# A graph layer with linear attention and routed experts: preparation and layers joined in one block, five of 49 tiles aggregated earlier

## The reference, cut to what matters

```python
xn = layernorm(x)
# graph branch
h   = xn @ W_gcn
deg = segment_sum(edge_weight, dst) + 1;  dinv = rsqrt(deg)
agg = segment_sum(dinv[src] * w * dinv[dst] * h[src], dst) + dinv**2 * h
g   = relu(0.5 * (layernorm(agg + b) * gamma + beta) + 0.5 * xn)
# linear attention, 8 heads
q, k, v = elu(xn@Wq)+1, elu(xn@Wk)+1, xn@Wv
att = (q @ (k.T @ v)) / (q @ k.sum(0)) @ Wproj + bproj
x1  = x + g + att
# 16 experts, the best two of each node, a last layernorm, and the residual
out = x1 + layernorm(xh + moe(xh)),  xh = layernorm(x1)
```

## Time and profile before

| what | value |
|---|---|
| median of 3 runs | 1736.85 us (1732.56 to 1738.45) |
| the profiled execution's own time | 1734.48 us |
| its span, first to last instruction | 1732.2 us |
| TensorE busy, its weight loads, VectorE, ScalarE, GpSimd | 84%, 70%, 59%, 29%, 58% |
| mean granted TensorE clock | 0.903 of full speed |
| first gather issued, last gather issued | 133.63 us, 1183.12 us |

### The profile page before, as it was taken

The page is one execution under the profiler, slowest core; times in us unless marked ns, Lnnn a source line. Parts: engine busy times, 40 slices in busy tenths (PEclk is TensorE's granted clock), DMA queues, the critical chain, the costliest instruction groups (busy, mean ns, idle before and its releaser), DMA issues. The chain is left out here.

```text
span 1732.2 us, 31432 instructions
## 1 busy us (share of the span) xinstructions
PE 1451.3 (84%) x8024; PEld 1205.2 (70%) x8025; DVE 1025.7 (59%) x3853; ACT 504.7 (29%) x1380; POOL 999.4 (58%) x1058
## 2 busy tenths in 40 slices
PE   5779979887968787977888869868499999999996
PEld 3668867665757565766666657645299999989975
DVE  8866367446367553852755528436755555566658
ACT  1346622121212111211111202101444444444424
POOL 0007037777777777777777777772045554545547
PEclk8889989897979888899888988878799999999998
DMA  7445113333333333333333333333932233254267
GB/s 241 157 149 183 59 44 104 106 105 104 107 104 104 107 104 107 104 106 105 107 104 107 104 107 104 106 105 92 216 113 77 71 123 97 73 170 149 76 216 279
DMA packets 107070, 207.62 MB, mean 120 GB/s; under 512 B 24496, under 2 KB 60080, under 8 KB 106960
## 3 DMA queue, kind: packets, MB, share of 16 engines
q0 software_dynamic: 48240, 131.91, 26.2%
q1 hardware_dynamic: 58720, 74.37, 14.0%
HBM read 172.60 MB, written 33.60 MB: 119 GB/s over the span
## 5 line engine op out<-in xcount | busy, mean ns | idle before, releaser
L137 POOL DMA_INDIRECT ring<-table,src x782 | 746.0, 954 | 437.7 <-issue 220.9
L1167 PE MATMUL bank<-ring,hots 128*128 x1372 | 321.7, 390 | 40.0 <-SPq L824 40.0
L1167 PEld LDWEIGHTS bank<-ring,hots 128*128 128x128 f32 x1372 | 264.5, 195 | 88.4 <-issue 51.8
L1674 ACT ACTIVATE one<-bank,b 128x128 f32<-128x128 f32 x424 | 155.5, 367 | 217.4 <-PE bank L1701 193.8
L1167 PE MATMUL bank<-ring,late_hots 128*128 x384 | 136.8, 508 | 93.4 <-SPq L824 87.0
L1701 PEld LDWEIGHTS bank<-one,w 128*128 128x128 f32 x1696 | 207.0, 193 | 8.1 <-issue 2.0
L1701 PE MATMUL bank<-one,w 128*128 128x128 f32 x1696 | 208.1, 276 | 1.3 <-issue 0.7
L1709 PE MATMUL bank<-w,one 128*128 128x256 f32 x848 | 202.8, 382 | 1.7 <-DVE y L1773 1.7
L1620 POOL DMA_INDIRECT spread<-y,to_x x109 | 107.2, 983 | 162.1 <-DMA spread<-y,to_x 82.9
L993 DVE TENSOR_SCALAR hots<-iota_t,edge_l 128x128 f32<-128x128 f32 x686 | 183.0, 362 | 1.8
L1167 PEld LDWEIGHTS bank<-ring,late_hots 128*128 128x128 f32 x384 | 91.0, 250 | 132.5 <-issue 117.9
(11 more groups left out here) (295 smaller groups left out, 2172.0 us busy)
## 6 DMA issues: line engine op xcount, KB each, us to landing
w<-in_w SPq DMA_DIRECT2D x32, 512.0 KB, 4.6
ring<-table,src POOLq DMA_INDIRECT x782, 2.8
xt<-in_x_cols SPq DMA_DIRECT2D x24, 512.0 KB, 4.0
got<-spread SPq DMA_DIRECT2D x11, 1024.0 KB, 10.4
rows<-xn SPq DMA_DIRECT2D x1, 6272.0 KB, 28.0
out<-xn SPq DMA_DIRECT2D x12, 512.0 KB, 5.3
x<-in_x SPq DMA_DIRECT2D x4, 896.0 KB, 9.4
table<-xn SPq DMA_DIRECT2D x1, 2048.0 KB, 8.9
```

The source lines that it names most:

```text
L137: return pool.indirect_dma_start(out=m.ring[:, b % RING, :], out_offset=None, in_=a.table, in_offset=bass.IndirectOffsetOnAxis(ap=m.src[:, ...
L1167: last = nc.tensor.matmul(agg, hot[:, k, :], two[:, k, :], start=False, stop=False)
L1674: act.activation(hT[:, fc, :], up_ps[fc], ACT.Relu, bias=b1[:, fc, bass.ds(i * SLOTS + slot, 1)]).then_inc(h_ok, 1)
```

## The change

- `prepare` and `layers` become one block, `graph`. Their buffers are laid over each other by hand in one tensor, `work` (`Area`).
- The keys and the context of the first 12 tiles (`TAIL`) move into the first half: line 1186 (`scored`) multiplies with 512 columns there instead of 256, ScalarE makes `kcur`, `nk`, `pk` and `ek`, and GpSimd adds `ek` and `pk`. The second half has 37 tiles left.
- The degrees come in five parts, with the last one 6 tiles instead of 10. ScalarE scales three tiles at a time after each tile and issues the stores of the first four parts itself. SyncE's queue keeps the loads of `xt`, now two tiles at a time into three slots; in the second half ScalarE issues them.
- Tiles 0, 1 and 2 are visited among the keys, after the products of tiles 28, 35 and 42 (`VISITS_AFTER`). Tiles 3 and 4 are visited in turns -2 and -1. Turn t visits tile `AGG[t]`, which is t + 5 at first. Turns 8, 16, 24, 32 and 40 (`PAUSES`) visit none, so that the lead falls by one at each and turn 48 visits tile 48.
- The aggregated rows are kept in `m.xn` and their moments in `mv` for each tile, since up to five tiles are ahead.
- The ring keeps its 32 batches, and GpSimd's loop of gathers is as it was. The number of visits, gathers and products is the same.

```diff
-PART_ENDS = (9, 18, 23, BATCHES)
+PART_ENDS = (8, 15, 21, 25, BATCHES)
+TAIL = 12
+XT_SLOTS = 3
+PAUSES = (8, 16, 24, 32, 40)
...
-        if part != BASE:
+        if part == LATE:
...
+        SEEDS_AFTER = {AT[q] + 4: q for q in range(FINAL)}
+        SCALED_AFTER = {AT[q] + 6: q for q in range(FINAL)}
+        LOADS = -(-NT // 2)
+        ALL_LOADS = LOADS + -(-(NT - TAIL) // 2)
+        SUMS_AFTER, FLAG_AFTER = TAIL + 3, TAIL + 14
+        VISITS_AFTER = {TAIL + 16: 0, TAIL + 23: 1, TAIL + 30: 2}
+        FIRST_TURN, LAST_TURN = -3, NT + 4
+        rows_left = iter(range(len(VISITS_AFTER), NT))
+        AGG = {t: next(rows_left) for t in range(FIRST_TURN + 1, NT) if t not in PAUSES}
+        assert AGG[LAST] == LAST and AGG[LAST - 1] == LAST - 1
...
+            for b in range(GATHERED_AHEAD, FULL):
+                if b >= RING and b % 2 == 0:
+                    pool.wait_ge(freed, (b + 2 - RING) // 2 + CREDIT)
+                gather(pool, m, a, b).then_inc(landed[b % RING // 4], 16)
...
+                dve.tensor_tensor(kk[:, t % 3], ek[:, t % 2], pk[:, t % 2], ALU.add).then_inc(kk_ok, 1)
+
+            tiles = iter(range(TAIL, NT))
 
             def between():
-                keys(next(tiles))
+                scaled_keys(next(tiles))
...
+            def built_early(t, hooks):
+
+                if t > 0:
+                    dve.wait_ge(iota_ok, t)
+                first, _, _, _, _, _, _ = pairs_of(dve, t)
+                slot = t % 2
+                dve.tensor_copy(edge[:, slot, 0, :], m.dst[:, bass.ds(first * 2, 2 * EARLY)])
+                dve.tensor_copy(edge[:, slot, 1, :], m.w[:, bass.ds(first * 2, 2 * EARLY)]).then_inc(edge_ok, 1)
+                dve.wait_ge(edge_ok, t + 1)
+                for j in range(2 * EARLY):
+                    last = dve.tensor_scalar(hots[:, slot, j, :], iota_t[:, slot, :], edge[:, slot, 0, j:j + 1], edge[:, slot, 1, j:j + 1],
+                                             ALU.is_equal, ALU.mult)
+                    if j in hooks:
+                        hooks[j]()
+                last.then_inc(early_ok, 1)
+
+            def moved_on(t):
+
+                dve.tensor_scalar(iota_t[:, t % 2, :], iota_t[:, t % 2, :], float(2 * P), None, ALU.add).then_inc(iota_ok, 1)
...
+            def aggregated(t):
+
+                r = Count(dve, chain_h, t * CHAIN_H, CHAIN_H)
+                dve.wait_ge(agg_ok, t + 1)
+                dve.scalar_tensor_tensor(tile(m.xn, t), agg_of(t), m.dinv[:, t:t + 1], m.vecs[:, V_B:V_B + D],
+                                         ALU.mult, ALU.add).then_inc(h_ok, 1)
+                dve.wait_ge(h_ok, t + 1)
+                r.add(dve.bn_stats(st[:, 0, :], tile(m.xn, t)))
+                r.wait()
+                r.add(dve.bn_aggr(mv[:, t, 0, :], st[:, 0, :]))
+                r.end()
...
+            built_early(0, {3: between, 8: between})
+            built_late(0)
+            moved_on(1)
+            built_early(1, {2: between, 6: lambda: aggregated(0), 7: between, 10: between, 13: between})
+            keys_to(TAIL + 22)
+            built_late(1)
+            moved_on(2)
+            built_early(2, {2: between, 6: lambda: aggregated(1), 7: between, 10: between, 13: between})
+            keys_to(TAIL + 29)
+            built_late(2)
+            moved_on(3)
+            built_early(3, {2: between, 6: lambda: aggregated(2), 7: between, 10: between, 13: between})
+            for t in tiles:
+                scaled_keys(t)
+
+            dve.wait_ge(ctx_mm, NT)
...
+            dve.wait_ge(ld_rest, 48)
+            c.add(dve.tensor_scalar(m.half, m.half, 0.5, None, ALU.mult))
...
-                if on(t, -1) and later(t, 0):
-                    dve.tensor_scalar(iota_t[:, o, :], iota_t[:, o, :], float(2 * P), None, ALU.add).then_inc(iota_ok, 1)
-                if on(t, 0) and not (t == LAST):
-                    built_late(t, n)
+                if t + 1 in AGG and later(t, FIRST_TURN + 1):
+                    moved_on(AGG[t + 1])
+                if t in AGG and not (t == LAST):
+                    built_late(AGG[t])
...
-                if on(t, 1):
-                    c = Count(dve, chain_h, (t - 1) * CHAIN_H, CHAIN_H)
-                    dve.wait_ge(agg_ok, t)
-                    dve.scalar_tensor_tensor(h[:, o], agg_ps[o], m.dinv[:, bass.ds(t - 1, 1)], m.vecs[:, V_B:V_B + D],
-                                             ALU.mult, ALU.add).then_inc(h_ok, 1)
...
-                if on(t, -1):
-                    if later(t, 0):
-                        dve.wait_ge(iota_ok, t + 1)
-                    built_early(t + 1, o)
+                if t - 1 in AGG:
+                    aggregated(AGG[t - 1])
+                if t + 1 in AGG and later(t, FIRST_TURN + 1):
+                    built_early(AGG[t + 1], {})
...
+                    left += [(part, t, min(t + 3, t1)) for t in range(t0, t1, 3)]
+                if left:
+                    scaled(*left.pop(0))
+            seeds(len(PARTS) + FINAL, *DEGREES[FINAL])
+            for some in left:
+                scaled(*some)
+
...
+            for t in range(NT):
+                pe.wait_ge(hw_ok, t + 1)
+                scored(t, t // 2, t % 2, 0 if t < TAIL else D, 2 * D)
+                if 2 <= t < TAIL + 2:
+                    context(t - 2)
+                if t in AFTER:
+                    degrees(AFTER[t])
+            pe.wait_ge(hw_ok, NT + 4)
+            for t in range(TAIL, NT):
+                if t >= TAIL + 4:
+                    pe.wait_ge(ek_ok, t - 3)
+                scored(t, LOADS + (t - TAIL) // 2, (t - TAIL) % 2, 0, D)
+                if t >= TAIL + 2:
+                    context(t - 2)
+                if t == SUMS_AFTER:
+                    pe.wait_ge(ready, 2)
...
+                if t in VISITS_AFTER:
+                    if VISITS_AFTER[t] == 0:
+                        pe.wait_ge(hs_ok, DEGREES[FINAL][0])
+                        pe.wait_ge(last_ok, NT - DEGREES[FINAL][0])
+                        pe.wait_ge(flag_ok, 2)
+                    aggregate(VISITS_AFTER[t])
+            context(LAST - 1)
+            context(LAST)
...
-                    summed_up(t - 1, 1 - n, tile(m.xn, t - 1))
-                if on(t, 0):
-                    first, soon, end, late, last, base, ended = pairs_of(pe, t)
-                    if later(t, 2):
-                        pe.wait_ge(h_ok, t - 1)
-                    nc.tensor.matmul(agg, m.ident, tile(m.xn, t), start=True, stop=False)
-                    if t == LAST:
...
+                    summed_up(t - 1)
+                if t in AGG:
+                    aggregate(AGG[t])
+
+            pe.wait_ge(h_ok, len(VISITS_AFTER))
...
-            turn(-2, 1)
+            turn(-3, 1)
...
-            turn(-1, 0)
+            turn(-2, 0)
...
+            pe.wait_ge(start_ok, 3)
+            turns(turn, -1)
...
-        with ExitStack() as graph:
-            graph_memory(nc, graph, m)
-            prepare(nc, m, a)
-            layers(nc, m, a)
+        with ExitStack() as held:
+            graph_memory(nc, held, m)
+            graph(nc, m, a)
```

1277 lines of the change are left out of this document (627 added, 650 removed).

## The result

| | before | after |
|---|---|---|
| median | 1734.7 us (1731.8 to 1738.45, 4 runs) | 1657.82 us (1656.13 to 1658.32, 4 runs) |
| the profiled execution, its span | 1734.48, 1732.2 us | 1656.13, 1654.3 us |
| first gather, last gather | 133.63, 1183.12 us | 121.86, 1105.87 us |
| from the first to the last | 1049.5 us | 984.0 us |
| from the last to the end | 549.1 us | 548.4 us |

The ratio after to before is 0.9552, with an interval of 0.9535 to 0.9568.

What follows compares the result with a forecast made beforehand. The prediction took GpSimd's issuing of gathers, 1.257 us each, as the bound from 241 to 1183 us, with VectorE nearly always busy before. It summed 1734.48 - 7 - 61 = 1666.5, forecast 1667 us, range 1648 to 1696.

Steps and rivals of the forecast that it cites:

- Part 1: Before the first gather: preparing gets shorter, -7 us, first gather at about 126.5; bounds -16 and +4.
- The waits: VectorE's waits in the first 128 us, 17.4 us: 3.4 stay, 13 of the other 14 are removed.
- The 2 us for loads that share the DMA engines with a store: First half: 2 us put back against the removed waits, as loads of `xt` share DMA engines with a store.
- The price of 6 for the 12 tiles: First half: GpSimd's 12 additions hold VectorE for 6 us, with 3 us of TensorE lying beside it.
- The shorter tail: Last part of degrees, 6 tiles: scaling 1.1 us less; smaller last store and shorter tail 2 us more.
- Part 2: GpSimd's idle stretch after the 32nd gather falls from 66.5 to 5.5 us: -61 us; bounds -66.5 and -45.
- Part 3: The turns: gathers stay the pace despite turns without visits, so 0 us; upper bound 25 us.
- Part 4: What costs nothing: ScalarE's issues of `xt`, gathers beside keys at 1.25 us, unchanged work after the last gather.
- A: Rival: the ring fills, GpSimd stands 15 to 40 us more, time 1682 to 1706; chance 0.19.
- B: Rival: preparing is not shorter, TensorE's work and GpSimd's holds eat the gain, 1673 to 1678 us; chance 0.13.
- C: Rival: the turns become the pace, deciding from 18.8 us a turn; slower by 63 us, 1798; chance 0.04.
- D: Rival: visits among the keys wait for the keys' end, idle time stays, 1727 us; chance 0.02.

## Why the prediction was right, and where it was off

**The bound.** GpSimd's issue of gathers was what set the end, in every kernel on the chips where before takes 1735 us. Each us of its idle time was one us of the total: 22.4 and 21.5 without visits, 7.7 and 8 at the handover. After it the distance to the end stayed, 548.4 for 549.1; in the single executions of the other kernels there it is 544 to 551.

**Part 1** said -7 and measured -11.8. Split at the start of VectorE's last scaling, 124.19 before and 113.35 after, it is -10.8 and -0.9, where the terms of the prediction give -3.5 and -3.1. The mechanism was right, the loads that stood behind stores; the sizes of four terms were not.

*The waits.* 13.7 of VectorE's 17.4 us went, but they are not the 13 of 14 that the prediction removed. It let 3.4 us stay because they come after the last batch of degrees, and most of them went. VectorE before and after:

```profile
122.19 0.18 DVE L467 TENSOR_TENSOR deg<-deg,bank 128x30 f32<-128x30 f32 x1 [3.36 <-PE bank L635]
...
111.39 0.17 DVE L650 TENSOR_TENSOR work<-work,bank 128x18 f32<-128x18 f32 x1 [0.55 <-PE bank L1173]
```

So 2.8 went there and 10.9 of the other 14. The 14.6 us of TensorE's waits for `xt`, to which the prediction traced them, were 8.7: the last 5.90 come after all of them. That the sum of the waits came out so near is in part luck.

*The 2 us for loads that share the DMA engines with a store* did not come in after: its first half has no wait for `xt` left, and its 1.5 us are at the start of the keys. The kernel without visits, with the same program there, does wait for loads in its first half, 3.2 us, and starts its last scaling 3.4 us later. So a part of the difference between -7 and -11.8 is scatter: the four kernels with this program have their first gather 7.9 to 12.2 us ahead of the one execution of before.

*The price of 6 for the 12 tiles* was near the measured 4.65 (113.35 against about 108.7 with 4 tiles and with none, within the same scatter), but not for its reason. The prediction had taken TensorE's lateness as covered. In the trace about half of the price is VectorE's waits for TensorE (0.5 and 2.1), which are in the 3.7 above already, and the holds alone are 2.3 us: 1.7 in the small one-hots (10.7 us, against 9.0 without additions) and 0.56 in one small operation (0.73 us instead of 0.17).

*The shorter tail* gave 0.9 where the prediction had 1.1 and 2. Its upper bound of +4 was no sum of its terms either: with no wait gone and both prices full, 1.5 - 1.1 - 2 + 8.7 + 3 is about +10.

The Trainium skill says in SBUF — State Buffer, section Who interferes with whom, that an instruction of VectorE with two inputs in SBUF and one of GpSimd that reads SBUF exclude each other for their whole length. By it VectorE could have been charged with 12 x 0.72 = 8.6. The runs agree that one waits for the other, as an addition of 2.96 us shows, but most of the waiting was GpSimd's, and VectorE's share was 0.19 us for each of 12 additions and 0.30 to 0.36 for each of 36.

**Part 2** said that 5.5 us of the 66.5 would stay, and none did. The step that failed is the time of the handover: the first pair of tile 3 was free at T + 96 instead of T + 107. Three terms were too large: the intervals between visits, 24 us each, were 20.4, since the 2.5 us given to VectorE lay beside TensorE's keys and the visits take 8.2; from tile 2's close to the keys' end it was 12.7 instead of 15.5, for the same reason; and from there to the tile's start 4.5 instead of 7.5. One was too small: tile 0's visits waited 5.41 us for VectorE's first one-hots, where the prediction had 3 for these, the flag and the branch together, and closed at T + 36.8 instead of T + 34.5. Together these are the 10.7 us by which tile 3 started early. The deadline was 1.7 us off the other way, T + 99.8 instead of T + 101.5, because tile 3 begins in the pair of batch 46 and not with batch 48. The rule itself, that GpSimd idles by what the first pair is late, gave the 7.7 us of the kernel with 4 tiles.

**Part 3** said 0, and was right. A turn without visits takes 7.2 us of TensorE's time where the prediction had 4.5 at least and put 10. GpSimd waited nowhere around them. From first to last gather 984.0 us passed, under the 990 that would have spoken against it. The place named as the risk, a turn without visits shortly before a long one, with TensorE 38 of 40 us behind, did not get so far. Counted in the same way, from the issue of a tile's first batch to its first visit, TensorE was 31 us behind at tile 14 (first visit at 433.69) and 30 at tile 41, which left 8 and 10 us before GpSimd wanted the place. The closest point of the whole kernel is tile 3 at the handover, with 36 us behind and 4 left.

**Part 4** held: the gathers beside keys are 1.25 us apart.

**The rivals.** A did not occur in after, but its mechanism did in the kernel with 4 tiles and three visits. B, with preparing no shorter, is excluded by 121.86. C's condition, turns that are slower than the gathers, holds on the other chips, where a turn takes some 24.9 us in place of 20: above the 18.8 from which it was to decide. There the four kernels with 12 tiles and five pauses, which differ little from after, took 0.3 to 1.5% less than before, and those with six and seven pauses no less than before or 1% more. So the loss of 63 us that C forecast did not come there either. After itself was not run there. D is excluded.

## What to carry to other kernels

Where one engine issues transfers into a ring at a fixed pace, the time is its first issue, plus its issues, plus its idle time, plus a fixed rest; so write down for each slot when it is wanted and when it is free, for the first slot of a block and not only for the last. Work in the way of the first visits can be put behind them, as far as each slot's deadline allows, and a saving ahead of the first issue is worth its full length only as long as the deadlines still hold. A store that has to wait and the loads that feed the bound engine belong on different queues.

## What the runs showed of the hardware that was not expected

- Between VectorE's float16 operations of 2.0 us with two inputs, an addition on GpSimd (0.72 us alone) took 0.73 to 2.96 us, and VectorE lost 0.30 to 0.36 us for each when 36 came close together, 0.19 when 12 came apart.
- Two chips ran the kernels 300 us and more longer, and not in proportion. Up to 120 us the times are the same within the scatter above, and visits without gaps take the same 7.93 us for 36 matmuls. After it TensorE, ScalarE and VectorE stand at times, with nothing named that they wait for: in the kernel with three turns together, among the keys, for 13.1, 15.4 and 9.4 us at the longest, and TensorE in the turns between single matmuls. The mean granted clock from 250 to 1100 us is 0.77 there (five turns together) against 0.88 in after; whether it is a cause or follows from the standing was not tested. From a kernel with four visits among the keys (L1208 are visits):

```profile
478.96 0.58 PE L1208 MATMUL bank<-ring,work 128*128 x1 [1.73 <-issue]
481.07 0.58 PE L1208 MATMUL bank<-ring,work 128*128 x1 [1.52 <-issue]
```

What makes an instruction late there was not found.
